# A graph kernel on one core: the setup stage in another order, table stores on the SP queue, edge rows in smaller groups

## What is computed

```python
def attention_layer(Z, U, Dmat, head_w, edges):        # K=4 heads, R=16
    ZU = einsum('nd,kdr->knr', Z, U)                    # 3125 x 64 numbers: the "sources"
    logits = (ZU[:, src] * ZU[:, dst]).sum(-1) / 4
    alpha = softmax of logits over the edges of one dst
    agg = segment_sum(alpha * ZU[:, src], dst)
    Z_half = 0.5 * Z + 0.5 * einsum('k,knr,kdr->nd', softmax(head_w), agg, U)
    ...                                                 # dense 256 x 256 step, relu
def gru_layer(h, rel, w_ih, w_hh, b_ih, b_hh, edges):
    red = segment_sum(h[src] + rel[kind], dst)
    return gru_cell(red, h)                             # gates of 768 columns
h = relu(layernorm(x)); x = x + attention_layer(h, ...)
h = relu(layernorm(x)); x = x + gru_layer(h, ...)
```

## Time and profile before

| | us |
|---|---|
| median of 3 runs | 1112.35 (1110.08 to 1118.23) |
| the profiled execution | 1117.96 |
| its span | 1115.9 |
| PE / DVE / ACT / POOL busy | 810.7 / 650.1 / 424.5 / 640.3 |

### The profile page before, as it was taken

One profiled execution on the slowest core, in us unless ns is written; L12 is line 12 of the kernel. 1 busy time (PEld: TensorE's weight loads), 2 busy tenths in 40 slices (PEclk: granted clock), 3 DMA queues, 4 the chain that ended last, 5 costly groups with the idle time before them and its releaser, 6 DMA issues.

```text
span 1115.9 us, 14910 instructions
## 1 busy us (share of the span) xinstructions
PE 810.7 (73%) x5278; PEld 575.4 (52%) x5278; DVE 650.1 (58%) x1208; ACT 424.5 (38%) x765; POOL 640.3 (57%) x943
## 2 busy tenths in 40 slices
PE   4833466777776655665566565757999999999996
PEld 4722354455544433444444443535777777777774
DVE  4351664655554444455455444645888878888852
ACT  3523233334344333333333333414444444444441
POOL 4688888888888888888888888840000000000000
PEclk9966656767776667667766676679999999999998
DMA  8262335344443434334334333111111111111111
GB/s 188 63 142 58 71 81 120 84 95 86 98 94 97 103 83 89 83 87 96 87 85 95 86 85 87 42 32 42 65 51 47 46 51 48 51 51 56 47 46 35
DMA packets 46513, 85.26 MB, mean 76 GB/s; under 512 B 11246, under 2 KB 29299, under 8 KB 43309
## 3 DMA queue, kind: packets, MB, share of 16 engines
q1 hardware_dynamic: 28898, 66.88, 18.7%
q0 software_dynamic: 16480, 17.31, 12.6%
q10 hardware_dynamic: 1056, 0.07, 0.1%
HBM read 67.29 MB, written 16.80 MB: 75 GB/s over the span
## 4 chain that ended last, share of the span: by engine, by line
POOL 55%; PE 31%; issue 8%; DMA 2%; DVE 2%; SPq 1%; ACT 1%; ACTq 0%; POOLq 0%; DVEq 0%
POOL shared L698 27%; POOL cnt_rows L703 15%; POOL zs_third L698 13%; PE bank L1866 12%; PE bank L1865 6%; PE bank L1892 4%; PE bank L1846 4%; PE bank L1893 2%; DMA layer<-in_edges,row_at 1%; PE bank L1808 1%; SPq L463 1%; SPq L465 1%; PE bank L1889 1%; DMA shared<-in_edges 1%; PE bank L1884 0%
## 5 line engine op out<-in xcount | busy, mean ns | idle before, releaser
L698 POOL DMA_INDIRECT shared<-zu_table,src_col x306 | 301.7, 986 | 53.8 <-issue 49.8
L703 POOL MEMSET cnt_rows<- 54x300 f32 x450 | 165.0, 367 | 0.4
L698 POOL DMA_INDIRECT zs_third<-zu_table,src_col x144 | 143.3, 995 | 23.5 <-issue 23.5
L1772 PE MATMUL bank<-layer,oh 128*125 128x84 f32 x900 | 134.7, 291 | 9.5 <-issue 5.1
L1772 PEld LDWEIGHTS bank<-layer,oh 128*125 128x125 f32 x900 | 120.0, 203 | 21.3 <-issue 14.1
L1010 DVE TENSOR_TENSOR layer<-shared,bank 128x512 f32<-128x512 f32 (+1 forms) x51 | 28.2, 554 | 154.3 <-DMA shared<-zu_table,src_col 115.8
L1754 PE MATMUL bank<-ident,L 128*72 128x128 f32 x75 | 19.2, 382 | 128.1 <-DVE L L1013 121.2
L965 DVE TENSOR_TENSOR shared<-iota_b,key_col 128x1500 bf16<-128x1500 bf16 (+2 forms) x47 | 88.5, 1883 | 0.0
L1808 PE MATMUL bank<-whhT,h2T_own 128*125 128x512 f32 x100 | 88.1, 979 | 0.0
L965 DVE TENSOR_TENSOR oh<-iota_b,low_col 128x3125 bf16<-128x3125 bf16 x25 | 85.2, 3410 | 0.0
L1754 PEld LDWEIGHTS bank<-ident,L 128*72 128x72 f32 x75 | 9.4, 150 | 133.7 <-DVE L L1013 125.3
(11 more groups left out here) (233 smaller groups left out, 1718.0 us busy)
## 6 DMA issues: line engine op xcount, KB each, us to landing
shared<-in_edges SPq DMA_DIRECT2D x25, 1125.0 KB
own_table<-own_out SPq DMA_DIRECT2D x25, 375.0 KB
shared<-own_table SPq DMA_DIRECT2D x25, 375.0 KB
shared<-zu_table,src_col POOLq DMA_INDIRECT x306
h_table<-h2s SPq DMA_DIRECT2D x25, 125.0 KB
h2s<-h_table SPq DMA_DIRECT2D x25, 125.0 KB
out_dram<-layer SPq DMA_DIRECT2D x25, 125.0 KB
xs<-in_x SPq DMA_DIRECT2D x5, 560.0 KB
```

The costliest lines, as they stand in the source:

```text
L698: nc.gpsimd.indirect_dma_start(out=zs[t % 3][:, j * KR:(j + 1) * KR], out_offset=None, in_=zu_table, in_offset=bass.IndirectOffsetOnAxis(a ...
L703: nc.gpsimd.memset(idle, 0.0).then_inc(idle_set, 1)
L1772: last = mm(ps(5, W, 0, SUMS), oh[:, h, j * W:(j + 1) * W], V[:, j, :], start=j == 0, stop=j == C - 1)
```

## The change

- `x`'s first five windows are loaded ahead of the destination rows. The three copies of these (425 wide each, six DMAs) become one load of 555 columns in two DMAs, out of which three views are taken; the semaphore `l_next` goes.
- DVE's stages of the setup stand in another order: `stats(0)` before the search, `find_edges` after `stats(4)` and `shifts(3)`. `find_rows` is split in two around `shifts(0)`. PE's `find_starts` comes after window 15 in place of window 9, and ACT's `scales(1)` to `scales(4)` come behind windows 3, 6, 11 and 16.
- The ten stores of `zu_table` leave POOL's queue for SP's, between the row loads.
- Row groups are 3, 9, 9 and 4 windows (before 9, 9 and 7). Two blocks of the second group are loaded early. The first gather of a window that begins a group waits for that group, so there is such a wait at windows 3, 12 and 21 (before 9 and 18).
- `few_dst` and `few_src` count on semaphores of their own, and `check_fives` waits for the five of `few_dst` alone; `make_keys` waits for the others.
- PE turns group 0 before the first 256 x 256 products of the dense step. The memsets in the gather stream stay.

```diff
-        dcur = part(W, at, EF, int32)
-        dnext = part(W, at + 512, EF, int32)
-        dfar = part(W, at + 1024, EF, int32)
+        d_all = part(W, at, EF + HALO_EDGES + 2, int32)
+        dcur, dnext, dfar = (d_all[:, a:a + EF] for a in (0, 1, HALO_EDGES + 1))
...
-        GROUPS = [(a, min(a + GRP, NW)) for a in range(0, NW, GRP)]
+        FIRST = 3
+        early_rows = FIRST + 2
+        GROUPS = [(0, FIRST)] + [(a, min(a + GRP, NW)) for a in range(FIRST, NW, GRP)]
+        GROUP_AT = {a: g for g, (a, b) in enumerate(GROUPS)}
+        COLUMN_BANK = (5, 6, 7, 5)
...
+            def store_sources(i):
+                a, b = fives_of(i)
+                sp.wait_ge(v_zu, i + 1)
+                for lo, hi in SIXTEENTHS:
+                    sp.dma_start(zu_table[a * W:b * W, :].rearrange("(t p) d -> p t d", p=W)[lo:hi, :, :], zus[lo:hi, a:b, :]
+                                 ).then_inc(st_zu, 16)
+
             load_x(0)
-            load_x(1)
-            load_rows_of_edges(1, dnext, l_next)
-            load_rows_of_edges(HALO_EDGES + 1, dfar, l_next)
-            for i in range(2, 5):
+            load_rows_of_edges()
+            for i in range(1, 5):
                 load_x(i)
...
+            store_sources(0)
+            store_sources(1)
             sp.wait_ge(starts_ready, 1)
-            load_rows(sp, 0)
+            load_rows(sp, 0, *GROUPS[0])
+            store_sources(2)
+            store_sources(3)
+            load_rows(sp, 1, FIRST, early_rows)
+            store_sources(4)
...
-                if t % GRP == 0:
-                    pool.wait_ge(a_col, 3 * (t // GRP) + 1)
+                if t in GROUP_AT:
+                    pool.wait_ge(a_col, 3 * GROUP_AT[t] + 1)
...
             find_rows()
             find_edges()
-            for i in range(5):
-                a, b = fives_of(i)
-                pool.wait_ge(v_zu, i + 1)
-                for lo, hi in SIXTEENTHS:
-                    pool.dma_start(zu_table[a * W:b * W, :].rearrange("(t p) d -> p t d", p=W)[lo:hi, :, :], zus[lo:hi, a:b, :]
-                                   ).then_inc(st_zu, 16)
             way(pool, windowed, by_blocks)
...
-            for i in range(5):
-                if i < 4:
-                    scales(i + 1)
-                act.wait_ge(v_nmr, i + 1)
-                for t in range(*fives_of(i)):
-                    normalise(t, t % 2)
-                    if t:
-                        keep_turned_rows(t - 1, 1 - t % 2)
-                if i == 2:
+            SCALES_BEHIND = {3: 1, 6: 2, 11: 3, 16: 4}
+            for t in range(NW):
+                if t % FEW == 0:
+                    act.wait_ge(v_nmr, t // FEW + 1)
+                normalise(t, t % 2)
+                if t:
+                    keep_turned_rows(t - 1, 1 - t % 2)
+                if t in SCALES_BEHIND:
+                    scales(SCALES_BEHIND[t])
+                if t == 18:
```

More of the change, by code:

```diff
@@ L263, in gnn_kernel @@
         l_small = sem("l_small")
-        l_rows = [sem(f"l_rows{g}") for g in range(3)]
+        l_rows = [sem(f"l_rows{g}") for g in range(4)]
         l_gru = sem("l_gru")
@@ L334, in gnn_kernel @@
         v_at = sem("v_at")
-        g_few = sem("g_few")
+        g_few_dst = sem("g_few_dst")
+        g_few_src = sem("g_few_src")
         v_over = sem("v_over")
@@ L458, in each_window, with load_rows @@
                 body(t, t // 2, t % 2)
-        def load_rows(eng, g):
-            for t in range(*GROUPS[g]):
+        def load_rows(eng, g, a, b):
+            for t in range(a, b):
                 first = eng.value_load(starts[0:1, t:t + 1], min_val=0, max_val=E)
@@ L495, in _, with load_rows_of_edges @@
         def _(sp):
-            def load_rows_of_edges(off, to, loaded):
+            def load_rows_of_edges():
                 for lo, hi in SIXTEENTHS:
-                    sp.dma_start(to[lo:hi, :], edges[1, FRONT + off:FRONT + off + E].rearrange("(p f) -> p f", p=W)[lo:hi, :]
-                                 ).then_inc(loaded, 16)
+                    sp.dma_start(d_all[lo:hi, :], bass.AP(edges.tensor, EP + FRONT + lo * EF,
+                                                          [[EF, hi - lo], [1, EF + HALO_EDGES + 2]])).then_inc(l_dst, 16)
             def load_x(i):
@@ L768, in find_edges @@
                 pool.wait_ge(v_at, 2)
-                for at, to in ((dst_at, few_dst), (src_at, few_src)):
+                for at, to, landed in ((dst_at, few_dst, g_few_dst), (src_at, few_src, g_few_src)):
                     for c in range(FIVES):
@@ L1583, in windowed @@
                 keep_turned(0)
-                keep_columns(1)
-                keep_columns(2)
+                for g in (1, 2, 3):
+                    keep_columns(g)
                 overlapped(attend)
@@ L1672, in _, with turn_rows_of_edges @@
             mm(ps(6, 1, 0, FIVES + 1), ones[0:W, :], flags[:, :], start=True, stop=True).then_inc(p_over, 1)
+            def turn_rows_of_edges(g):
+                a, b = GROUPS[g]
+                for t in range(a, b):
+                    rows = late_rows[:, (t - FIRST) * 128:(t - FIRST + 1) * 128] if g else rows_f[:, t * 128:(t + 1) * 128]
+                    last = tr(ps(COLUMN_BANK[g], 128, (t - a) * 3 * C, (t - a + 1) * 3 * C), rows,
+                              ident[0:3 * C, 0:3 * C])
+                last.then_inc(p_col, 1)
+            pe.wait_ge(a_rowf, 1)
+            turn_rows_of_edges(0)
             pe.wait_ge(l_dense, 48)
@@ L1679, in _ @@
             last.then_inc(p_gd, 1)
-            def turn_rows_of_edges(g):
-                a, b = GROUPS[g]
-                for t in range(a, b):
-                    rows = late_rows[:, (t - GRP) * 128:(t - GRP + 1) * 128] if g else rows_f[:, t * 128:(t + 1) * 128]
-                    last = tr(ps(5 + g, 128, (t - a) * 3 * C, (t - a + 1) * 3 * C), rows,
-                              ident[0:3 * C, 0:3 * C])
-                last.then_inc(p_col, 1)
-            pe.wait_ge(a_rowf, 1)
-            turn_rows_of_edges(0)
             pe.wait_ge(v_zu, 5)
```

64 lines of the change are left out of this document (35 added, 29 removed).

## The result

| | before | after |
|---|---|---|
| median, us | 1114.55 (1110.08 to 1118.65, 6 runs) | 1101.54 (1096.36 to 1104.91, 6 runs) |
| profiled execution, us (its span) | 1117.96 (1115.9) | 1102.19 (1100.3) |
| first gather at, us | 57.87 | 46.42 |
| first to last gather, us | 681.7 | 677.6 |
| last gather to the end, us | 376.3 | 376.2 |

The ratio is 0.9875, with a 95% interval from 0.9839 to 0.9912. The change is 13.0 us faster by the medians, against 10.7 forecast. The interval (0.9 to 1.6%) lies on both sides of the 1% that I had named as the bound.

The account below looks back on a forecast made before the run. It took POOL's unbroken stream of 450 gathers, with a fixed distance from first gather to end, as the bound. First gather 57.87 to 46.7, less 0.5 for collision, takes 10.7 off 1112.35: 1101.7 us, range 1097 to 1108.

Parts of the forecast that it names:

- What bounds the kernel: POOL's 450 gathers are one unbroken stream, so the end stands at a fixed distance behind the first gather, 57.87 us.
- Three strands: Setup: columns (about 43.5), table (46.7) and POOL's own queue (about 44.5); the first gather follows the latest.
- x first, -5.0 us: Setup: with x loaded first, ACT normalises its first window at 8.5 in place of 13.54.
- Slips of +1.0 on the way to the last sources: ACT's wait for third statistics and PE's for `find_edges`: +1.0 us for both (0.5 to 2); last sources at 41.3.
- The found rows unmoved within 1.5 us: Setup: the found rows, asked for some 2 us later, still land within 1.5 us of before (25.45).
- The late search: Rival, 20%: found rows land 4 us later (29.4), first gather at 50.1, 7.3 us off, 1105.1.
- The starts at 30.3: Setup: `find_starts` behind window 15 gives the starts at 30.3 in place of 34.23.
- SP's queue: Setup: three row blocks done at 36.6, four store DMAs 1.9 to 3.0 us, last landing 45.7 or 47.0, first gather 46.7.
- The collision, +0.5: First gathers: DVE's chain for the dense step's matrices newly falls beside gathers and slows them, +0.5 us (0 to 1.5).
- Window 3 waits for nothing: Stream: V of window 0 stays near 127.6 (124 to 129), ahead of window 3's gather at about 133.9; cost 0.
- The stream unchanged at 681: From the first gather on: a stream of 681 us, unchanged; growth of more than 2 us would be wrong.
- The sum: Whole kernel: 57.87 - 46.7 - 0.5 = 10.7 us off, median 1101.7; the forecast holds 53%.

Follow-up runs that it names:

- the first series: Four kernels, each the changed kernel with one part undone: 1151.97, 1158.35, 1160.1 and 1156.37 us, beside the kernel before at 1155.37 us.
- last store first: The changed kernel with the last store of zu_table ahead of the two early row blocks on SP's queue: 1100.4 us, ratio 0.9858.
- the second loading: The changed kernel without memsets and with the last store ahead of the two early row blocks, loaded again unchanged: 1380.1 us, ratio 1.2038.

## Why the prediction was right, point by point

- **What bounds the kernel.** Right. The end followed the first gather: stream and tail kept their lengths to 4.1 and 0.1 us, and the kernels that keep the memsets, DVE's new order and the stores on SP had, outside the first series, a stream of 677.5 to 677.7 us, wherever it started.
- **Three strands, the latest decides, and it is the table.** Right: the release was a DMA to the table. The columns were complete at 41.9 (43.5 forecast), and POOL was done with the edge gathers at 43.35. The experiments moved the lead as the sums said: to the columns (groups of nine: 54.72 and 54.76), to POOL's own queue (last store first: 44.88), and back to the table. The parts don't add: 8.3, 7.0, 2.3 and 5.4 us are each what is lost when the others stay.
- **x first, -5.0 us.** Mis-sized: -4.25 (13.54 to 9.29). I had x in at 5.1 us by the moved bytes; it landed at 6.3. The two loads of destination rows, 0.28 MB, are issued right behind it, at 1.74, and by 6 us the DMAs had moved 0.92 MB, which is x's first five windows (0.64 MB) and these rows together. So the sum left out the bytes that travel beside x; that they are the cause is worked out, not tried by a run.
- **Slips of +1.0 on the way to the last sources.** They came out at -0.2: -10.80 in all, less the -4.25 and the -6.35 of the stall. That 40.87 came out so near 41.3 is luck: this error and the one on x nearly cancel.
- **The found rows unmoved within 1.5 us.** Right: 24.85 against 25.45. The late search, 20% of my chances, did not happen.
- **The starts at 30.3.** 31.2: the products behind window 15 began at 29.95, where I had 29.5, and the last conversion took 0.62 us in place of 0.18.
- **SP's queue.** The three blocks were issued by 37.2 (36.6 forecast), four stores took 1.88 us (1.9 to 3.0), the last store was issued at 44.03 and landed in 2.12 us, not 2.6. The choice of the x load as the nearest row, 0.47 us, was right: a store on SP took 0.44. The first gather was at 46.42 against 46.7.
- **The collision, +0.5.** Not seen. The gathers' row, grouped as the earlier trace rows, of the first 13 after:

```profile
L711 POOL DMA_INDIRECT shared<-zu_table,src_col x13 | 15.9, 1225 | 5.0 <-DMA zu_table<-zus 3.1 <-issue 1.9
```

  1225 ns against 1219. But the premise was wrong too: the chain of the dense step's matrices on DVE ran beside gathers before the change as well (57.81 to 61.8, behind a first gather at 57.87) and does so after it (48.12 to 53.2), so nothing new came to lie beside them. The four gathers beside it after the change took 0.95 to 0.96 us each, so the chain held none of them up, and the 1.5 us that stood beside the Trainium skill's rule of the port pair which VectorE and GpSimd share ("SBUF — State Buffer", Who interferes with whom) was not paid. The long gathers lie elsewhere. POOL's row of the longest, after, and DVE's row beside it:

```profile
63.33 2.69 POOL L711 DMA_INDIRECT shared<-zu_table,src_col  x1 [0.16 <-issue]
62.63 2.56 DVE L960 SCALAR_TENSOR_TENSOR oh<-iota_w,win_first,dst_col 128x2250 f32<-128x2250 f32 x1 [0.65 <-PE bank L1726]
```

  No run here shows that the one instruction held the other up.
- **Window 3 waits for nothing.** Right: V of window 0 ended at 122.6, 10.1 us ahead of the gather at 132.74. I had it unmoved at 127.6, between 124 and 129; the weights' long issue began 10.1 us earlier and was shorter (9.81 us against 13.08).
- **The stream unchanged at 681.** Wrong by 4.1 us, the largest error of the sum, and more than the 2 us that I had named for a longer stream. Outside the first series, the kernels in the old order or with the stores on POOL had streams of 679.3 to 681.7, the changed ones 677.5 to 677.7. So about 2 us go with the change, and the rest looks like scatter of the one profile before. The 450 gathers were busy for 441.8 us in place of 445.0, and the idle time between them was 71.8 in place of 73.3; nothing here isolates the cause.
- **The sum.** 10.7 forecast; 0.3 more at the first gather, 0.5 for the collision that did not come, and the shorter stream make 15.6 in the profiles, 13.0 in the medians. That the predicted 1101.7 is so near to the measured 1101.54 is luck: the gain was 2.3 us larger than forecast, and the kernel before was 2.2 us slower in these runs, 1114.55, than in the three earlier ones, 1112.35. I had put "within 1%" ahead of "faster by over 1%"; it came out at 1.25%.

The best of the kernels run is the one without memsets, 1002.36 us. A twin with one store moved falls to 1370, so it would have to be proven in more loadings before use. Of those that keep the memsets, the last store first (ratio 0.9858) and the change itself (0.9875 and 0.9864) aren't told apart.

## What to carry to other kernels

When several strands meet in one wait, write down when each ends, and credit an edit only up to the next strand: moving the stores alone gave 0, and in the full change it is worth 6 us, even where nothing large is sent beside them. Look at what the moved work was holding back on the other queue: here the stores on SP also kept 2.2 MB of broadcasts, and what follows them, behind them, which was worth more (9 us of first gather) than the issue on POOL (5.4). A start that moves a stream which nothing else bounds comes back whole at the end; a stream that waits inside, as in the first series, seems to swallow it, though the change itself wasn't measured there.

## What the runs showed of the hardware

- A gather behind a memset starts after 0.16 us of idle, a gather behind a gather after 0.30. A memset of 0.37 us between two of them costs only 0.22.
- Ten small stores (16 and 140 KB) released the gather 1.8 us after the last issue with nothing large ahead of them, and 10.9 us after it with two broadcasts of 1.1 MB and the first weights behind them sent meanwhile.
- In one order of instructions without memsets, while gathers went out PE issued a product only each 2.80 us at the worst, where 54 had taken 3.04 us, at unchanged gathers of 0.95 us. That worst stretch is of the second loading; gaps of up to 2.5 us between two of the attend sums stood in both, 1370 and 1380 us, and in the profiles of no other kernel to that extent: the idle before the attend sums that waits for nothing was 262 and 280 us there and at most 20 elsewhere.
